# Moving sixteen elementwise multiplications from VectorE to GpSimd in the last stage of a two-layer decoder

## What is computed

```python
def _L1_ffn_ref(x, proj_w, proj_b, expert_bias, fc1_w, fc1_b, fc2_w, fc2_b, sh1_w, sh1_b, sh2_w, sh2_b):
    ...
    topk_w, topk_idx = jax.lax.top_k(probs, K)          # 2 of 8 experts per token
    ...
    kept_w, kept_pair = jax.lax.top_k(wmat, cap)        # at most cap tokens per expert
    ...
    h = jax.nn.gelu(jnp.einsum('ecd,ehd->ech', xe, fc1_w) + fc1_b[:, None, :], approximate=False)
    oe = jnp.einsum('ech,edh->ecd', h, fc2_w) + fc2_b[:, None, :]
    contrib = oe * kept_w[..., None]
    y = jnp.zeros((N, Cx), x.dtype).at[kept_tok.reshape(-1)].add(contrib.reshape(-1, Cx))
    sh = jax.nn.gelu(xf @ sh1_w.T + sh1_b, approximate=False) @ sh2_w.T + sh2_b
    return ((sh + y) * FC_MULT).reshape(Bx, Tx, Cx)
```

## Time and profile before

| | |
|---|---|
| median of 3 runs | 783.79 us (778.82 to 784.41) |
| the profiled execution | 783.95 us, of which its span 782.2 us |
| mean granted clock of TensorE | 0.965 of full speed |
| first spread transfer of stage 5 issued | 706.17 us |
| first multiplication of chunk 2 on DVE | 710.54 us |
| last scaling on DVE begins | 778.68 us |

### The profile page before, as it was taken

The page is one execution under the profiler, slowest core; times in us unless marked ns, Lnnn a source line. Parts: engine busy times, 40 slices in busy tenths (PEclk is TensorE's granted clock), DMA queues, the critical chain, the costliest instruction groups (busy, mean ns, idle before and its releaser), DMA issues.

```text
span 782.2 us, 18700 instructions
## 1 busy us (share of the span) xinstructions
PE 712.6 (91%) x7706; PEld 374.3 (48%) x7706; DVE 472.1 (60%) x1102; ACT 396.5 (51%) x731; POOL 108.6 (14%) x103
## 2 busy tenths in 40 slices
PE   6899999997999979999976769999999799999996
PEld 3354545453655643444425445555566444444342
DVE  0663353525687857667557885566665476646772
ACT  2737473744767754424442233655654434555464
POOL 1280221211000000000014445211110000000000
PEclk9999999998999979999978999999999899999998
DMA  8400000000000004441300000000000000007530
GB/s 349 173 4 0 3 1 3 0 4 1 3 2 2 2 13 98 109 97 46 77 2 1 0 0 1 3 4 3 3 4 4 2 0 0 1 0 188 169 109 27
DMA packets 11634, 29.44 MB, mean 38 GB/s; under 512 B 1112, under 2 KB 1240, under 8 KB 11032
## 3 DMA queue, kind: packets, MB, share of 16 engines
q1 hardware_dynamic: 11552, 28.27, 12.4%
HBM read 27.02 MB, written 1.25 MB: 36 GB/s over the span
## 4 chain that ended last, share of the span: by engine, by line
PE 67%; DVE 14%; ACT 8%; issue 7%; DMA 2%; POOL 1%; DVEq 0%; SPq 0%; ACTq 0%
PE bank L1803 5%; PE bank L2335 4%; PE bank L1834 4%; PE bank L2345 3%; PE bank L2394 3%; PE bank L2385 3%; PE bank L2048 3%; PE bank L2036 3%; PE bank L2041 3%; PE bank L2170 2%; PE bank L1847 2%; PE bank L2231 2%; PE bank L2235 2%; PE bank L2177 2%; DVE sb_rowmax L1175 2%
## 5 line engine op out<-in xcount | busy, mean ns | idle before, releaser
L1803 PE MATMUL bank<-sb_xT,sb_arena 128*128 128x512 f32 x128 | 59.2, 611 | 6.9 <-DMA sb_arena<-w 6.9
L921 ACT ACTIVATE sb_arena<-bank 128x512 f32<-128x512 f32 x64 | 34.8, 606 | 49.3 <-PE bank L2201 49.3
L1493 DVE TENSOR_REDUCE sb_rowmax<-bank 128x4 f32<-128x512 f32 x64 | 41.2, 686 | 23.6 <-PE bank L2192 23.6
L650 ACT ACTIVATE sb_arena<-bank 128x512 f32<-128x512 f32 x64 | 36.1, 600 | 29.2 <-PE bank L1803 29.1
L1097 DVE TENSOR_TENSOR sb_arena<-bank,sb_arena 128x512 f32<-128x512 f32 x32 | 21.0, 687 | 46.0 <-PE bank L1847 46.0
L825 ACT ACTIVATE sb_arena<-bank 128x512 f32<-128x512 f32 x36 | 21.5, 598 | 48.8 <-PE bank L2036 46.8
L565 POOL TENSOR_TENSOR sb_arena<-sb_la,sb_consts 128x1024 f32<-128x1024 f32 x16 | 31.4, 1972 | 91.0 <-PE bank L1834 71.0
L1803 PEld LDWEIGHTS bank<-sb_xT,sb_arena 128*128 128x128 f32 x128 | 24.9, 196 | 38.1 <-issue 36.4
L2036 PE MATMUL bank<-sb_xT,sb_w 128*128 128x512 f32 x72 | 37.9, 609 | 0.0
L2048 PE MATMUL bank<-sb_arena,sb_w 128*128 128x512 f32 x72 | 36.1, 601 | 1.6 <-DVE sb_arena L1394 1.4
L2041 PE MATMUL bank<-sb_xT,sb_w 128*128 128x512 f32 x72 | 37.0, 595 | 0.0
(11 more groups left out here) (328 smaller groups left out, 1586.6 us busy)
## 6 DMA issues: line engine op xcount, KB each, us to landing
sb_arena<-weights_by_expert SPq DMA_DIRECT2D x16, 512.0 KB, 8.1
sb_w<-weights_by_expert SPq DMA_DIRECT2D x32, 256.0 KB, 3.5
sb_w<-w SPq DMA_DIRECT2D x1, 2646.5 KB, 22.3
sb_w<-w SPq DMA_DIRECT2D x1, 1736.0 KB
sb_consts<-consts SPq DMA_DIRECT2D x1, 1275.0 KB, 10.7
sb_arena<-w SPq DMA_DIRECT2D x2, 512.0 KB, 6.0
sb_ctxT<-ctx SPq DMA_DIRECT2D x1, 1024.0 KB, 12.5
out<-sb_xT SPq DMA_DIRECT2D x4, 256.0 KB, 3.4
```

Of the source, the lines that this page charges most:

```text
L650: act.activation(BC[:, n, :], bank[(4, 5, 0, 1)[n % 4]][:], ACT.Copy).then_inc(s_vev, 1)
L921: act.activation(probT4[k % 2][:, g].rearrange("p b j q -> p (b j q)"), by_key[g][:], ACT.Exp).then_inc(s_e4, 1)
L1493: dve.tensor_reduce(rowmax4[k % 2][:, 4 * g:4 * g + 4], bank[n][:].rearrange("p (j t) -> p j t", j=4), AX, ALU.max).then_inc(s_mx4, 1)
L1803: pe.matmul(bank[(4, 5, 0, 1)[n % 4]][:], bc_w_tiles[:, n, :], cols(c), start=True, stop=True).then_inc(s_v, 1)
```

## The change

The 16 multiplications of `add_ahead5` are issued by POOL, in a new function `stage5` behind its stage 4, in the same order and into the same two buffers. DVE keeps the 16 additions. The semaphores are the same: POOL waits for the result computed ahead (`s_eo`), for the spread weight, and for the addition that read the buffer two before (`s_ca`); DVE waits for the multiplication (`s_cm`).

```diff
@@ gpsimd
+        def stage5():
+            for c in range(AHEAD):
+                for e in range(E5):
+                    k = E5 * c + e
+                    spread, landed, count = spread_at(EARLY, c, e)
+                    wait(pool, s_eo, k + 1)
+                    wait(pool, landed, count)
+                    wait(pool, s_ca, k - 1)
+                    pool.tensor_tensor(weighted5[k % 2], out5[k], spread, ALU.mult).then_inc(s_cm, 1)
+
         setup_pool()
         run(pool, [front0, front1, front2, front3], [no_pre, no_pre, no_pre, pre3], [tail0, tail1, tail2, tail3], [nothing] * 4)
         stage4()
+        stage5()
@@ vector
         def add_ahead5(c, e):
             k = E5 * c + e
-            wait(dve, s_eo, k + 1)
-            spread, landed, count = spread_at(EARLY, c, e)
-            wait(dve, landed, count)
-            wait(dve, s_ca, k - 1)
-            dve.tensor_tensor(weighted5[k % 2], out5[k], spread, ALU.mult).then_inc(s_cm, 1)
             wait(dve, s_cm, k + 1)
             wait(dve, s_ca, k)
             total = shared_x[:, bass.ts(c, CHUNK)]
             dve.tensor_tensor(total, total, weighted5[k % 2], ALU.add).then_inc(s_ca, 1)
```

## The result

The changed kernel takes 785.2 us in the median of 20 runs (783.7 to 790.4), the kernel before 783.8 us in 20 runs (777.8 to 785.8). The ratio is 1.0046, 95% interval 1.0026 to 1.0065: slower by 3.6 us (2.0 to 5.1), within the 1% that I called "no change", but not zero. The forecast was 786.7 us, within 1%.

The account below looks back on a forecast made before the run. DVE was taken to bound the first half of chunk 2. Down products 7 and 8 gave +2.9 us, chunk 2's end and SP's queue 0: 783.95 to 786.85 us profiled, 786.7 median; range for 8 in 10, 782.5 to 790.5.

Parts of the forecast that it names:

- What bounds the kernel: Stage 5, first half of chunk 2: DVE is full, 1.93 to 1.94 us a step against PE's 1.72.
- What is to be gained: If POOL's part cost nothing, PE gets back 0.47 us in the first steps and 0.72 at chunk 2's end: 1.2 us.
- DVE and POOL exclude each other: Stage 5, two SBUF operands on both engines: one served at a time, a step 2.32 us in place of 1.93.
- The order of turns: Chunk 2: POOL served after each DVE instruction gives the upper value at down product 8, POOL pushed back the lower, +2.6.
- The third case of the earlier trace: Stage 3, at 444.49 us: POOL's instruction, issued before DVE's second, yet went behind it and ended 1.12 us later.
- The sum: Chunk 2, eight POOL multiplications among DVE's: down product 7 at 728.5 us, +2.7; down product 8 +3.1; +2.9 taken.
- The end of chunk 2: DVE queue before down product 14: loses a 0.72 us multiplication, but POOL's next may take 1.12 us; 0 taken.
- SP's queue and chunk 3: SP's queue waits for the same semaphores, cost 0; chunk 3 keeps the same PE gaps, all shifted.
- The signs in the profile: Chunk 2: POOL multiplications 1.6 us or more, L1722 and L1708 partly 1.6 to 1.8, multiplication 8 about 729, clock 1.00.
- POOL is hidden: Rival, stage 5: POOL's 1.28 us fit in a PE step, so 782.6 us; chance 0.10, including DVE only slightly disturbed.
- Strict turns with handovers: Rival, chunk 2: POOL never ahead, each step a chain of 2.65 us, about 790.5 us in all; chance 0.13.
- The clock falls: Rival, the eight steps of chunk 2: PE's clock at 0.59, each step 2.9 us, 791.5 us in all; chance 0.05.

Follow-up runs that it names:

- The kernel with memsets: Changed kernel with each of POOL's 16 multiplications replaced by two memsets of the same buffer, same waits and signal; 783.12 us, ratio 0.9988 against the kernel before.
- alone: Kernel before plus eight extra multiplications on POOL in chunk 2 that nobody waits for, DVE's own work unchanged; 792.25 us, ratio 1.0101.

## Why the prediction was right

- **What bounds the kernel** (DVE in the first half of chunk 2): right. PE's waits from 712.79 to 724.18 are all for L1722.
- **What is to be gained, 1.2 us**: right. The kernel with memsets gained 1.15 in the profile.
- **DVE and POOL exclude each other, 0.60 and 1.12 us, step 2.32**: right. Measured 0.60 and 1.07, step 2.28, in the changed kernel and alone (3.00 against 1.93). From the start of DVE's multiplication 0 to the end of multiplication 7, 17.96 us were predicted and 18.01 measured (708.39 to 725.72 + 0.68). A little of this closeness is luck: POOL's first two, in a row, took 2.50 us (709.09) and not 2 x 1.12, and the six behind them 1.07 each. Multiplication 8 was put at 730.8 at its end, if POOL got in again, which is 20.26 us after multiplication 0; it was 20.29.
- **The order of turns**: I took the middle between POOL getting each turn by issue order and POOL being pushed back. In stage 5 the first issued went first each time, and no instruction of POOL was pushed back. The third case of the earlier trace rows remains as the only exception.
- **The sum, "+2.7 us at down product 7, +3.1 at 8, taken +2.9"**: the right mechanism, mis-sized; measured +4.03. I read the loss at down products 7 and 8, as 728.5 minus 725.84. But down product 7 didn't wait for DVE before. It stood behind an up product and the bias product, and its multiplication had long been done. Of the kernel before, PE and DVE:

```profile
722.87 1.13 PE L2394 MATMUL bank<-sb_arena,sb_w 128*128 128x512 f32 x2
...
724.79 1.12 PE L2390 MATMUL bank<-sb_arena,sb_w 8*128 8x512 f32 x2
...
722.13 0.69 DVE L1716 TENSOR_TENSOR sb_arena<-sb_arena,sb_w 128x512 f32<-128x512 f32 x1
...
724.06 0.68 DVE L1716 TENSOR_TENSOR sb_arena<-sb_arena,sb_w 128x512 f32<-128x512 f32 x1
```

  The multiplication of 722.13 is done at 722.82 and down product 6 starts at 722.87: this is where PE waits. The one of 724.06 is done at 724.74, and down product 7 starts 1.10 us later. The loss belongs to down product 6: 710.54 + 13 x 0.60 + 7 x 1.12 = 726.18 against 722.87, **+3.3**. The slack ahead of down product 7 had been counted as if it could absorb part of the loss, but PE is late already when it comes there. The other 0.7 us: DVE's multiplication 0 started 2.35 us after the first up product and not 1.78, **+0.57**. Its transfer ended that wait, not ACT. This is scatter of the profiled runs, whose programs are the same up to there: eight of the twelve kernels had 1.78, the kernel before among them, and four had 1.92, 2.20, 2.35 and 2.48, each ended by the transfer. Of the last 0.15, 0.13 is that the sum lets PE go on 0.60 us after multiplication 6 starts, and PE starts 0.73 us after it (723.45 to 724.18).
- **The end of chunk 2, "-0.7 to +0.4, taken 0"**: +0.33 (down product 14, the row with `x4`, started 3.47 us behind down product 12's start, 3.14 before; the wait is 1.49 against 1.15). POOL's multiplication, released by the addition, took its turn ahead of multiplication 14, the bad end of the two.
- **SP's queue and chunk 3, 0**: right, 31.00 us in all but the one with four buffers (31.25).
- **Total +2.9 us**: +4.37 in chunk 2, 3.8 of it without the 0.57 of scatter, and +3.6 (2.0 to 5.1) by the repeated runs. The bounds +1.5 to +4.6 held both values. That 786.7 us lies above the measured median of 785.2 although the term was too small comes from the scatter of the runs; that the median lies so near the forecast is luck.
- **The signs in the profile**: the additions at 1.75 us, the clock of 1.00 and the unchanged chunk 3 came as listed. L1722 did not: it kept 0.68 us up to step 9. POOL's multiplications from 712.30 us to the end of step 7 are recorded as 1.44 to 1.56 us, not 1.6 or more. PE's first wait lies at 712.79, ahead of the 715 given. And "about 729" for multiplication 8 is 18.5 us behind multiplication 0, where the prediction's own sum gives 19.7 and 19.61 was measured (728.00).
- **The rivals.** *POOL is hidden*: excluded by the additions of 1.75 us. *Strict turns with handovers*, a step of 2.65: excluded by 2.28 us and by the memsets, which pass through the same semaphores at no cost; only the first step (3.67 us, 708.39 to 712.06) looks like it, with DVE idle for 1.32. *The clock falls*: not here, it was 1.00 from 706 to 770 us. That it can was seen once, below.

## What to carry to other kernels

An idle POOL was no free engine here for elementwise work on two SBUF operands. Before such a move, ask whether DVE is busy with two SBUF operands at the same time, and if so, price the move at POOL's time on the path (here 1.07 us) against DVE's (0.72 us). In this kernel the move gained only where DVE itself waits for another engine, and more buffers made it no better. When a queue falls behind, read the loss where the consumer already waits for it in the trace of before; at a place where the consumer waits for something else, the difference of times counts slack that is no longer there.

## What I had not expected of the hardware

- A multiplication by a constant on POOL, one SBUF operand, is recorded as 2.00 us where two operands in the same place, also issued 0.05 us behind DVE's addition, are recorded as 1.77. Yet it costs DVE only 0.41 against 1.07. DVE's instruction ended while POOL's was still recorded as running, so for this form the two do not simply take turns. This rests on one profile.
- In the kernel with four buffers the granted clock fell. Busy time by stretch, columns as in the earlier trace rows:

```profile
713.00:717.00 4.00, 2.18 (x6) 0.63 (x4) 3.43 (x3) 1.70 (x3) 3.55 (x4) 1.00 0.54 107
717.00:719.00 2.00, 1.93 (x4) 0.68 (x4) 2.00 (x3) 0.00 (x0) 1.14 (x1) 0.87 0.27 89
719.00:721.00 2.00, 2.00 (x3) 0.84 (x3) 2.00 (x4) 0.69 (x1) 0.00 (x0) 0.50 0.83 262
```

  PE was busy for 2.18 of 4.00 us in 713 to 717, with a wait of 1.90 us for DVE at its end, and then worked at 0.50, the 1.2 GHz level, from 719 to 721. In the changed kernel PE was busy for 2.92 us of 712 to 716 and the clock stayed at 1.00, the 2.4 GHz level, as it did up to 770 us in the other eleven kernels. The fall cost nothing here, since PE caught up before down product 6 and waited for DVE again.
